# A transformer layer's setup: the head mixings of M and N done by one block-diagonal product over rows rearranged through DRAM

## The reference

```
scaled = num_value / 1000                      # 12,500 words; the first 250 are numbers
sin_table = sin(scaled[:, None] * (1..128))
h = where(is_num, sin_table, weight)[x]        # the table, looked up

dots = einsum('bhid,bhjd->bhij', q, k) * scale         # q = x Wq, k, v = x Wkv; H = 8, DH = 64
dots = where(eye, -1e-9, dots)
dots = einsum('bhij,hg->bgij', dots, mix_pre)
attn = softmax(dots)
attn = einsum('bhij,hg->bgij', attn, mix_post)
out  = concat_h(attn_h @ v_h) @ Wout
```

## Time and profile before

| | |
|---|---|
| median of 3 runs | 1504.01 us |
| profiled execution | 1516.0 us, its span 1514.3 us |
| setup block | 0 to about 64 us of the span |
| attention block | from 64.2 us |
| PE busy over the span | 1465.3 us (97%) |
| DVE, ACT, POOL busy | 69%, 76%, 63% |

### The profile page before, as it was taken

The page is one execution under the profiler, slowest core; times in us unless marked ns, Lnnn a source line. Parts: engine busy times, 40 slices in busy tenths (PEclk is TensorE's granted clock), DMA queues, the critical chain, the costliest instruction groups (busy, mean ns, idle before and its releaser), DMA issues. The chain is left out here.

```text
span 1514.3 us, 33889 instructions
## 1 busy us (share of the span) xinstructions
PE 1465.3 (97%) x11160; PEld 1339.9 (88%) x11160; DVE 1047.0 (69%) x2811; ACT 1146.8 (76%) x3477; POOL 959.1 (63%) x991
## 2 busy tenths in 40 slices
PE   5789999999999999999999999988999999999999
PEld 2469888888888988889888898877999999999999
DVE  7887788788777887778887787763344333356665
ACT  5589888888888888888888888865555555555555
POOL 7175567888788888788878877664677566510000
PEclk9999999999999999999999999999999999999999
DMA  7324511211211111111111111022244234456665
GB/s 237 132 73 163 164 38 49 69 48 42 60 38 39 55 42 36 35 56 34 36 56 34 37 38 48 26 60 67 69 116 106 70 71 109 120 158 190 189 184 146
DMA packets 171503, 126.48 MB, mean 84 GB/s; under 512 B 30309, under 2 KB 154959, under 8 KB 171330
## 3 DMA queue, kind: packets, MB, share of 16 engines
q1 hardware_dynamic: 153794, 104.15, 23.3%
q0 software_dynamic: 17536, 20.17, 4.8%
HBM read 61.64 MB, written 78.66 MB: 93 GB/s over the span
## 5 line engine op out<-in xcount | busy, mean ns | idle before, releaser
L1129 ACT ACTIVATE expd<-masked,nmax 128x128 f32<-128x128 f32 x1024 | 396.0, 393 | 0.3 <-DVE nmax L1282 0.3
L925 POOL TENSOR_TENSOR prob<-expd,rtotal 128x1024 f32<-128x1024 f32 x128 | 243.5, 1902 | 117.3 <-DVE rtotal L1251 115.8
L1265 DVE COPY_PREDICATED masked<-off_diag,ps_s 128x1024 f32<-128x1024 int32 x128 | 175.0, 1367 | 164.3 <-PE ps_s L1018 164.3
L1062 PE MATMUL ps_o<-u,probT 128*128 128x128 f32 x2048 | 249.0, 275 | 0.0
L1062 PEld LDWEIGHTS ps_o<-u,probT 128*128 128x128 f32 x2048 | 238.9, 191 | 0.0
L1129 ACT ACTIVATION_READ_ACCUMULATOR expd<-masked,nmax 128x1 f32 x1024 | 197.0, 192 | 0.0
L1138 ACT ACTIVATE u<-ps_ut 128x1024 f32<-128x1024 f32 x128 | 131.4, 1026 | 66.3 <-PE ps_ut L1073 66.3
L1227 DVE TENSOR_TENSOR w_lo<-ps_w,w_hi 128x512 fp32r<-128x512 f32 x256 | 164.3, 681 | 0.9 <-ACT w_hi L1167 0.9
L1167 ACT ACTIVATE w_hi<-ps_w 128x512 fp32r<-128x512 f32 x256 | 146.1, 595 | 15.7 <-PE ps_w L1048 9.3
L1158 ACT ACTIVATE probT<-ps_ut 128x1024 f32<-128x1024 f32 x128 | 131.4, 1027 | 33.9 <-PE ps_ut L1030 27.5
L1046 PE MATMUL ps_w<-xT_hi,M_hi 128*128 128x256 f32 x512 | 154.1, 301 | 3.0 <-DVE xT_lo L1221 2.2
(11 more groups left out here) (261 smaller groups left out, 3824.9 us busy)
## 6 DMA issues: line engine op xcount, KB each, us to landing
turned<-x2T SPq DMA_DIRECT2D x32, 256.0 KB, 2.2
answers_sp<-zeros SPq DMA_DIRECT2D x16, 512.0 KB, 4.3
answers_fq<-zeros SPq DMA_DIRECT2D x16, 512.0 KB, 3.8
xT<-turned SPq DMA_DIRECT2D x56, 128.0 KB, 2.3
sh_back<-answers_sp SPq DMA_DIRECT2D x56, 128.0 KB, 2.4
sh_back<-answers_fq SPq DMA_DIRECT2D x56, 128.0 KB, 2.5
out<-res SPq DMA_DIRECT2D x56, 128.0 KB, 2.1
h_sb<-in_L_tok_weight SPq DMA_DIRECT2D x12, 512.0 KB, 5.9
```

The source lines that it names most:

```text
L925: nc.gpsimd.tensor_tensor(prob[k % 2][:, :].rearrange("p (g j) -> p g j", g=H), expd[k % 2][:, :].rearrange("p (g j) -> p g j", g=H), rtot ...
L1062: mm = nc.tensor.matmul(ps_o[:, 0:D], probT[k % 2][:, g * N:(g + 1) * N], u[k % 2][:, g * D:(g + 1) * D], start=(g == 0), stop=(g == H - 1))
L1129: ins = nc.scalar.activation(expd[(k - 1) % 2][:, g * N:(g + 1) * N], masked[(k - 1) % 2][:, g * N:(g + 1) * N], ACT.Exp, bias=nmax[(k - 1 ...
L1265: nc.vector.copy_predicated(masked[k % 2][:, :].rearrange("p (g j) -> p g j", g=H), off_diag[:, :].unsqueeze(1).to_broadcast([P, H, N]), p ...
```

## The change

The products of the heads are no longer mixed before but after they are made. `by_heads(w)` makes on PE the eight 64-deep products Wk_h Wq_h^T (w = 0) and Wv_h Wout_h (w = 1), each 128x128, unmixed, into ps_m, even heads (partitions 0 to 63) in its first bank, odd ones (64 to 127) in its second. ACT copies them to SBUF (`cut`), SP writes them to the DRAM tensor `by_head` and reads them back as 16 rows times 8 heads on the partitions and 8 row groups times 128 columns along them (`heads_out`, `heads_in`). `by_bands(w)` multiplies by the block-diagonal `mixer` (128x128, 16 blocks of 8x8), ACT copies again, and the result goes through DRAM once more, back to its natural rows (`mix_out`, `mix_in`). From there ACT makes the high part (`high`) and POOL the low one. The 8 mixings on POOL are gone. Beside it: POOL fills `masked` and makes the turn constants, DVE does its thousandths in one pass and `kept` goes out ahead of the weights, the gather of the own rows comes after that of the own numbers, WARM is 6 instead of 13.

```diff
-            for c in range(2 * HC):
-                mix(c)
+            for w in range(2):
+                link.inc(nc.gpsimd.tensor_tensor(mixer[:, w, :].rearrange("p (a h) -> p a h", h=H), bands[:, :, :],
+                                        co[:, w, :].unsqueeze(1).to_broadcast([P, P // H, H]), ALU.mult))
+                made[f"mixer{w}"] = link.n
+            for k in range(2):
+                link.inc(nc.gpsimd.tensor_copy(masked[k][:, :].rearrange("p (g j) -> p g j", g=H),
+                                               diag[:, :].unsqueeze(2).to_broadcast([P, H, N])))
...
+            for w, n in enumerate("MN"):
+                pool.wait_ge(S["cut"], w + 5)
+                link.inc(nc.gpsimd.tensor_tensor(mats[n + "_lo"][:, :], parted[:, w, :], mats[n + "_hi"][:, :].bitcast(F32), ALU.subtract))
...
+        def bands_of(t):
+            return t.rearrange("(b a) (h j) -> (a h) b j", a=P // H, h=H)
...
+            def heads_out(w):
+                sp.wait_ge(S["cut"], w + 1)
+                sp.dma_start(by_head[w], whole_sb[:, w, :]).then_inc(S["mix_put"], 16)
+            def heads_in(w):
+                sp.wait_ge(S["mix_put"], 16 * (w + 1))
+                sp.dma_start(parted[:, w, :].rearrange("p (b j) -> p b j", b=H), bands_of(by_head[w])).then_inc(s_mix[w], 16)
+            def mix_out(w):
+                sp.wait_ge(S["cut"], w + 3)
+                sp.dma_start(bands_of(by_mix[w]), whole_sb[:, w, :].rearrange("p (b j) -> p b j", b=H)).then_inc(S["mix_put"], 16)
+            def mix_in(w):
+                sp.wait_ge(S["mix_put"], 16 * (w + 3))
+                sp.dma_start(parted[:, w, :], by_mix[w]).then_inc(s_mix[w], 16)
...
+            def cut(n):
+                act.wait_ge(S["M"], n + 1)
+                nc.scalar.activation(whole_sb[:, n % 2, :], ps_m[:, :], ACT.Copy).then_inc(S["cut"], 1)
+            def high(w):
+                act.wait_ge(s_mix[w], 32)
+                nc.scalar.activation(mats["MN"[w] + "_hi"][:, :], parted[:, w, :], ACT.Copy).then_inc(S["cut"], 1)
...
+                if c in (5, 7, 10, 11):
+                    cut((5, 7, 10, 11).index(c))
+                if c == CHUNKS - 1:
+                    high(0)
...
+            high(1)
...
+            def by_heads(w):
+                pe.wait_ge(S["wT_out"], 2 + w)
+                pe.wait_ge(S["numT_out"], 2)
+                need(pe, S["cut"], w)
+                for h in range(H):
+                    at = slice(h % 2 * DH, (h % 2 + 1) * DH)
+                    ins = nc.tensor.matmul(ps_m[:, h % 2 * 512 + h // 2 * D:h % 2 * 512 + (h // 2 + 1) * D], (wkT, wvT)[w][at, h // 2, :], mix_src[at, w * HC + h // 2, :],
+                                           start=True, stop=True)
+                ins.then_inc(S["M"], 1)
+            def by_bands(w):
+                pe.wait_ge(S["made"], made[f"mixer{w}"])
+                pe.wait_ge(s_mix[w], 16)
+                pe.wait_ge(S["cut"], w + 2)
+                for half in range(2):
+                    at = slice(half * 512, (half + 1) * 512)
+                    ins = nc.tensor.matmul(ps_m[:, at], mixer[:, w, :], parted[:, w, at], start=True, stop=True)
+                ins.then_inc(S["M"], 1)
...
+                if c == 4:
+                    turn(2)
+                    by_heads(0)
                 if c == 6:
...
+                    by_heads(1)
+                if c in (9, 10):
+                    by_bands(c - 9)
```

More of the change, by code:

```diff
@@ L57 @@
 AHEAD = 2
-WARM = 13
+WARM = 6
 CLEARS = B * N // P // CLEAR_ROWS
@@ L312, in setup @@
         mix_src = sb("mix_src", [P, 2 * HC, P])
-        mix_co = sb("mix_co", [P, HC, 2, H])
-        mixed = sb("mixed", [P, 2 * HC, H * D])
+        co = sb("co", [P, 2, H])
+        bands = sb("bands", [P, P // H, H])
+        mixer = sb("mixer", [P, 2, P])
+        whole_sb, parted = (sb(n, [P, 2, H * D]) for n in ("heads_sb", "parted"))
+        turn_rows = sb("turn_rows", [KR, 3, D])
         pre = sb("pre", [H, H])
@@ L331, in setup @@
         ps_c = pb("ps_c", 512)
-        names = ("made", "num", "isn", "ids0", "numbers", "kept", "small", "freq", "numbers0", "rows0", "stat0", "early_put", "num_f", "numT", "numT_out", "angle", "whole", "reduced", "turn", "sine", "done", "put",
-                 "weights", "wT", "wT_out", "coef", "coefd", "coef_out", "mixed", "M", "hi")
+        names = ("made", "num", "isn", "ids0", "numbers", "kept", "small", "freq", "numbers0", "rows0", "early_put", "num_f", "numT", "numT_out", "angle", "whole", "reduced", "link", "sine", "done", "put",
+                 "weights", "wT", "wT_out", "coef", "coefd", "coef_out", "M", "cut", "mix_put")
         S = {n: sem("s_" + n) for n in names}
         s_row = [sem(f"s_row{k}") for k in range(4)]
+        s_mix = [sem(f"s_mix{k}") for k in range(2)]
+        by_head = [nc.dram_tensor(f"by_head{w}", (P, H * D), F32).ap() for w in range(2)]
+        by_mix = [nc.dram_tensor(f"by_mix{w}", (P, H * D), F32).ap() for w in range(2)]
+        def bands_of(t):
+            return t.rearrange("(b a) (h j) -> (a h) b j", a=P // H, h=H)
         w_main = weight[0:P * VR, :].rearrange("(p r) d -> p (r d)", p=P)
@@ L457, in _ @@
                     continue
+                if i == 9:
+                    heads_out(0)
+                if i == 12:
+                    heads_in(0)
                 need(sp, s_row[i % 4], loaded.get(i - 4, 0))
@@ L469, in _ @@
             for i, c in enumerate(ORDER[:ON_TIME]):
+                if i == 2:
+                    heads_in(1)
+                if i == 4:
+                    mix_out(0)
+                if i == 6:
+                    mix_in(0)
+                    mix_out(1)
+                if i == 7:
+                    mix_in(1)
                 sp.wait_ge(S["done"], i + 1)
@@ L484, in _ @@
             nc.scalar.activation(nought[:, 1:2], nought[:, 0:1], ACT.Sin)
-            act.wait_ge(S["turn"], 1)
+            act.wait_ge(S["made"], made["turn"])
             for r in range(VC):
@@ L651, in halves @@
-                link.wait()
-                for part in (0, 2):
-                    ins = nc.vector.tensor_tensor(num_hl[:, chunks, 0:n, part + 1], src, num_hl[:, chunks, 0:n, part].bitcast(F32), ALU.subtract)
-                ins.then_inc(S["num_f"], 1)
+                src = part[:, 0, chunks.start * VC:chunks.start * VC + (chunks.stop - chunks.start) * n].rearrange("p (c r) -> p c r", r=n)
+                high, low = (num_hl[:, chunks, 0:n, k:PARTS:2] for k in range(2))
+                both = src.unsqueeze(3).to_broadcast([P, chunks.stop - chunks.start, n, 2])
@@ L676, in _ @@
+            halves(slice(0, CHUNKS - 1), VC)
             dve.wait_ge(S["small"], 16 * 4)
```

167 lines of the change are left out of this document (65 added, 102 removed).

## The result

1521.73 us median (13 runs, 1518.98 to 1525.38) against 1507.23 (13 runs) for the kernel before in the same comparison: ratio 1.0084, 95% interval 1.006 to 1.0108. The forecast was 1506.5 (1500.0 to 1511.5). The change is slower than any case that the prediction allowed for.

The account below looks back on a forecast made before the run. Setup was taken as bound by an 11 us PE hole cut by POOL's mixings, then PE's angles and products. New chain +1.3 us and low clock +1.2 gave +2.5 on the 1504.0 median: 1506.5 us, range 1500.0 to 1511.5.

Parts of the forecast that it names:

- the last of the sum: Whole kernel: profiled execution stands 12.0 us above the runs' median, so the +2.5 was added to 1504.0, giving 1506.5.
- The chain: Setup, up to POOL's N_lo: the new dependent steps end at 65.1 us against 63.77 before, +1.3.
- second copy done: Setup, ACT: the copy after by_heads(1) and angles 7 is through at 37.7 us.
- heads_in(1) issued: Setup, SP: goes out at about 42 us, after 3.0 us of small-load issue and 0.9 for two table writes.
- the two transfers by heads: Setup, DMA: heads_out(1) issued at 37.7 us; heads_in(1) out at about 42, behind two table writes, landing near 47.7.
- the prediction's rule on row groups: Setup, PE: products in different row groups overlap, so a by_heads costs 1.9 us at the low clock; sum 1505.8.
- the upper bound 3.75: Setup, PE: eight by_heads products at 0.47 us each at the low clock; 2.5 us was taken.
- rival (b): Setup, PE: by_heads takes 3.75 us both times, setup ends at 67.6, time 1509.0 us; chance 0.24.
- Rival (a): Setup, PE: high clock kept, stall's gain stays, setup ends near 61.3 us, time 1501.5; chance 0.25.
- The low clock: Attention's start, PE: first products take 0.42 us, not 0.28; charged 1.2 us, bounds 0 and 3.4.
- The DVE stall: Setup: DVE's third put, stalled 14.3 us by the mixings, 10.7 reaching PE, is freed; no 15 us instruction remains.
- Rival (c): End of setup: DVE's table part, not M and N, sets the end; 1499.4 us, or 1504 by chance; chance 0.08.

Follow-up runs that it names:

- lower heap: The faster of two groups of timed runs of the unchanged kernel before: seven of 13 at 1503.4 to 1507.2 us in the first comparison, median 1504.0.
- b_look2: Second further trace of the kernel before, nothing changed: 1503.68 us.
- b_hold: Kernel before with one added wait: DVE's third put waits until all 8 mixings on POOL are done; 1513.89 us, ratio 1.0073.
- b_turns: Kernel before with POOL's mixings waiting in turn for DVE's puts (last three together), small fills ahead of them; 1504.02, repeats 1504.64 and 1504.65 us.
- upper trace: The profiled execution of the unchanged kernel before that the prediction was made from: 1516.0 us.
- b_look1: First further trace of the kernel before, nothing changed: 1505.34 us.
- a_same: The changed kernel run once more, nothing altered: 1521.13 us (8 runs).
- a_same2: The changed kernel again, nothing altered, as a reference on one chip: 1519.96 us (4 runs).
- a_direct: Changed kernel without the DRAM route and the mixing, high and low parts cut from the unmixed products, so another output: 1504.93 us (10 runs).
- upper heap: The slower of two groups of timed runs of the unchanged kernel before: six of 13 at 1515.8 to 1517.1 us in the first comparison.

## Why the prediction was wrong

**The step that failed is the last of the sum: "That one stands 12.0 above the median of the runs; the median would be 1504.0 + 2.5 = 1506.5."** The new chain had been compared with a program that contained PE's hole of 10.66 us; the result was then added to runs that don't contain it. Measured from the lower heap, the removed stall is worth nothing, and the same sum would have given 1516.0 + 2.5 = 1518.5 for a kernel that has no such choice. b_look2 (start at 53.91), b_hold and b_turns show this. The wrong base is 12.0 of the 15.2 us. Of these 12.0 the stall is shown for about 10 (start 10.3 us later than in b_look2; 9.9 us when b_hold forces it); the other 2 lie behind the first gather (span less gather 1436.8 in the upper trace, 1435.1 and 1434.7 in b_look1 and b_look2), and their cause stays open.

**The chain was 3.1 us too short** (65.1 forecast, 68.2 measured; 63.77 before):

| term | forecast | measured |
|---|---|---|
| second copy done | 37.7 | 38.05 |
| heads_in(1) issued | 42 | 43.12, since heads_out(1) landed only then |
| heads_in(1) landed | 47.7 | 50.0: 6.9 us for 5.7 |
| by_bands(1), angles, fourth copy | 7.9 | 7.85 |
| mix_out(1), mix_in(1) | 3.0, 3.3 | 3.2, 3.6 |
| high(1), N_lo | 1.2, 1.90 | 1.1, 2.35 |

The structure was as described: PE waiting on `parted` ahead of by_bands(1), then all one behind another. **What was mis-sized are the two transfers by heads,** taken from rows of lone or half-size transfers: the write landed 5.0 us after its issue (38.08 to 43.12) where 3.0 at most was charged, and so, not SP's own issues, set when the read went out; the read took 6.9 for 5.7. The sum had two table writes ahead of the read; in the trace two more go out behind it at 43.53, and the engines are full. That the second copy came within 0.4 us is in part luck: the last number rows came at 32.02 in place of 30.8, and a quicker by_heads(1) made up some of it.

**by_heads** took 2.08 us at the low clock (the angles just ahead of it took 1.22 us a chunk), close to the 1.9 of the prediction's rule on row groups, and the upper bound 3.75 falls; no run makes the same products without the alternation. The 1505.8 given with that rule takes one by_heads 0.6 us shorter; by the count of rival (b), both, it would be 1505.3. It gained nothing: PE then waited 3.61 us for DVE's numbers. Rival (b) had the right sign by a mechanism that did not happen. Rival (a)'s own terms (3.2, 0.6 and 1.8 off 65.1) give an end at 59.5, not the 61.3 that it states; it didn't come about either way.

**The low clock** came as described, products at 0.41 in place of 0.28 us. It is read from these durations, the same as where the granted clock reads 0.50; from 71 to 76 us of this trace the profile gives 1.00. Charged 1.2; from start to gather it was 15.03 - 13.36 = 1.67 in this execution, and 1.2 and 1.3 in a_same and a_same2, so the charge was well sized.

**The DVE stall** is gone, as forecast; the two fills on POOL (27.45, 2.02 us in all) met no put, since none was due between 26.80 and 31.88; no full-size put of setup took more than 1.50.

Sum: the chain 3.1 and the clock 0.5 more than charged, +6.1 in place of +2.5 for the profiled execution. With the 12.0 of the base that is 15.6 us, against 15.2 seen, as the profiled execution stood 0.4 above its median. **Rival (c),** that the table's part sets the end once M and N are quick, isn't shown: a_direct, at 1504.9, ends with N's low part on POOL.

Behind the first gather nothing is explained by the change: span less gather is 1436.8 both before and after, and between 1433.5 and 1436.8 in all traces here. Two executions of one kernel can differ by as much (1436.8 after the change, 1433.9 in a_same), so a difference of 3 us between single traces is read from the start of attention, not from the time.

## What to carry to other kernels

When the profiled execution differs from the timed runs by about as much as the stall that a change removes, suspect that the timed runs don't have the stall, and take gains and losses from the same execution as the time they are added to. A trip through DRAM to rearrange data costs four waits in a row, not bytes alone: it can pay only where something else is waited for anyway. Here, in the lower heap, POOL's mixing cost nothing that leaving it out would have saved. Where one engine can shut out another, try to let them take turns by a semaphore: here that, together with a later first mixing, cost nothing in the median (1504.0 to 1504.7) and removed the bad case.

## What was not expected of the hardware

One DVE instruction lost to eight consecutive GpSimd instructions, not to one: 15.58 us for a put of 1.29 in the one traced execution of the upper heap, where 31 of 96 runs lie; in the two traced lower ones it got through in 1.63 us and the mixings stretched from 14.86 to 20.16. The Trainium skill, "SBUF — State Buffer", Who interferes with whom, tells of the wait for the instruction that is running; that the loser may be passed over again when that one ends is shown by the rows only. What decides it from run to run is not shown. The traces point at 0.3 us in the landing of `kept`, ahead of the mixings; why this differs stays open, as the same program showed 13 lower runs of 13 in one comparison and 17 upper of 23 in another.
